# Eight full expert units listed after tile 16 and run right behind the last sums of a graph and expert kernel

## What is computed

```python
edge_index = jnp.stack([src, dst])            # 3125 nodes of 256 numbers; E = 12500 edges are used
x = x + gnn(layernorm(x), edge_index, ...)    # two layers: mean over incoming edges @ W_l + x @ W_r + b
x = x + moe(layernorm(x), ...)                # 8 experts, the best 2 of each row

def moe(tokens, router_w, w1, b1, w2, b2):
    probs = softmax(tokens @ router_w.T)
    rw, re = top_k(probs, 2);  rw = rw / rw.sum(-1)
    out = tokens
    for e in range(8):
        h = gelu(tokens @ w1[e] + b1[e])      # 256 -> 256
        out = out + combine[:, e:e + 1] * (h @ w2[e] + b2[e])
```

## Time and profile before

| | us |
|---|---|
| median of 3 runs (range) | 593.08 (591.64 to 593.94) |
| profiled execution, its own time | 592.88 |
| its span from the first to the last instruction | 591.2 |
| PE busy in the span | 554.3 |
| DVE busy | 364.7 |
| ACT busy | 222.2 |
| POOL busy | 185.5 |

### The profile page before, as it was taken

One profiled execution on the slowest core, in us unless ns is written; L12 is line 12 of the kernel. 1 busy time (PEld: TensorE's weight loads), 2 busy tenths in 40 slices (PEclk: granted clock), 3 DMA queues, 4 the chain that ended last, 5 costly groups with the idle time before them and its releaser, 6 DMA issues.

```text
span 591.2 us, 11509 instructions
## 1 busy us (share of the span) xinstructions
PE 554.3 (94%) x3050; PEld 336.3 (57%) x3051; DVE 364.7 (62%) x1219; ACT 222.2 (38%) x422; POOL 185.5 (31%) x180
## 2 busy tenths in 40 slices
PE   4999999999999999999999999999991499999996
PEld 3555555555555555555445555555551488888885
DVE  5998667667657667663255766767678334444442
ACT  4676845434444434443101100000000155555554
POOL 3751000000000000000040154443356237787887
PEclk9999999999999999999999999999996799999999
DMA  8421211111111111012642146673332757787776
GB/s 259 148 79 60 65 45 54 48 34 54 44 37 55 37 44 54 28 55 53 196 129 80 55 137 200 202 245 126 106 130 97 228 109 118 125 142 129 129 116 92
DMA packets 64343, 61.24 MB, mean 104 GB/s; under 512 B 11281, under 2 KB 62334, under 8 KB 64302
## 3 DMA queue, kind: packets, MB, share of 16 engines
q1 hardware_dynamic: 47422, 44.84, 25.2%
q0 software_dynamic: 11200, 14.40, 13.1%
q10 hardware_dynamic: 5680, 1.49, 1.2%
HBM read 32.34 MB, written 29.30 MB: 104 GB/s over the span
## 4 chain that ended last, share of the span: by engine, by line
PE 69%; DMA 9%; DVE 8%; issue 8%; POOL 4%; SPq 1%; ACT 0%; POOLq 0%; DVEq 0%; ACTq 0%
PE bank L1306 22%; PE counts_ps L1448 8%; PE bank L1459 8%; PE bank L1221 8%; PE bank L1296 7%; PE counts_ps L662 7%; PE counts_ps L1306 4%; POOL xs_dram L593 2%; DMA rows<-in_x 2%; PE counts_ps L1439 2%; DMA xs_dram<-w,onehots 2%; DMA y<-y_dram 2%; PE bank L1211 1%; POOL stat L581 1%; PE bank L1289 1%
## 5 line engine op out<-in xcount | busy, mean ns | idle before, releaser
L1306 PE MATMUL bank<-y,adj 128*128 128x512 f16 x625 | 154.7, 379 | 0.4 <-ACT zt L1519 0.4
L1306 PE MATMUL counts_ps<-y,adj 128*128 128x512 f16 x625 | 144.0, 379 | 2.0 <-DMA y<-y_dram 2.0
L669 ACT ACTIVATE adj<-counts_ps 128x1000 f32 (+1 forms) x80 | 80.2, 1005 | 59.2 <-PE counts_ps L662 59.2
L635 POOL DMA_INDIRECT out<-adj x56 | 88.4, 1578 | 37.9 <-ACT adj L1654 18.5
L1306 PEld LDWEIGHTS counts_ps<-y,adj 128*128 128x128 f16 x625 | 60.7, 101 | 64.7 <-DMA y<-y_dram 4.3
L1306 PEld LDWEIGHTS bank<-y,adj 128*128 128x128 f16 x625 | 57.9, 97 | 59.5 <-issue 13.7
L565 POOL IOTA onehots<- 128x8 int32 x1 | 0.1, 143 | 225.4 <-PE counts_ps L662 225.4
L1448 PE MATMUL counts_ps<-adj 128*128 128x256 f32 x240 | 57.0, 380 | 0.0
L662 PEld LDWEIGHTS counts_ps<-onehots 125*128 125x128 f16 x640 | 42.4, 98 | 23.6 <-ACT adj L669 11.0
L648 DVE TENSOR_TENSOR onehots<-iota,lo_t 125x1024 f16<-125x1024 f16 x80 | 54.7, 684 | 1.8 <-issue 0.9
L1618 ACT ACTIVATE rows<-bank 128x256 f32<-128x256 f32 x25 | 9.6, 384 | 123.0 <-PE bank L1380 123.0
(11 more groups left out here) (237 smaller groups left out, 646.6 us busy)
## 6 DMA issues: line engine op xcount, KB each, us to landing
adj<-xs_dram SPq DMA_DIRECT2D x31, 264.0 KB
rows<-z_dram SPq DMA_DIRECT2D x49, 128.0 KB, 2.1
z_dram<-zt SPq DMA_DIRECT2D x33, 128.0 KB, 1.7
adj<-in_L_ffn_w SPq DMA_DIRECT2D x16, 256.0 KB, 3.2
rows<-in_x SPq DMA_DIRECT2D x24, 128.0 KB
out<-yo SPq DMA_DIRECT2D x24, 128.0 KB
y_dram<-yo SPq DMA_DIRECT2D x23, 128.0 KB, 1.7
y<-y_dram SPq DMA_DIRECT2D x4, 640.0 KB, 6.8
```

The source lines that it names most:

```text
L635: g.indirect_dma_start(out, bass.IndirectOffsetOnAxis(ap=ids[u][:, h:h + 1], axis=0), ye[u][:, h, :], None, bounds_check=N - 1, oob_is_err ...
L669: nc.scalar.activation(adj[:, :, bass.ds(at, GW * WD)].rearrange("p b (h d) -> p b h d", d=WD), counts_ps[:, 2 * (group % 2):2 * (group % ...
L1306: last = te.matmul(to, adj[:, b, t * P:(t + 1) * P], y[:, b, :], start=(b == 0), stop=(b == NT - 1))
```

## The change

A first list of eight units is made from the counts of the first 16 tiles: per expert as many units as are already full, the lowest experts first, until there are eight. DVE counts and lists behind tiles 18 and 19, PE spreads inside tile 21, DVE writes the first entries of the tables. The first two units' rows are loaded, and their weights and shares kept, during tiles 22 and 23. Behind the last matmul of tile 24 PE goes straight on to these eight units, and the routing of the last tiles, the second list (all other units) and the padding stand between their parts on every engine, written out by hand. The loops then run from unit 8 on. The 14 fillers go. The core of the difference follows.

On SP, the loads and paddings (the first two lines stand in tile 22, behind a wait for the scatters of 16 tiles):

```diff
+            load_rows(first_row, 0)
+            load_rows(second_row, 1)
...
+            next_rows(4, row_of(4))
+            row = row_of(5)
+            pad_expert(0)
+            next_rows(5, row)
+            row = row_of(6)
+            pad_expert(1)
+            pad_expert(2)
+            next_rows(6, row)
...
+            sp.wait_ge(S["table"], 2)
+            row = row_of(EARLY)
...
             sp.wait_ge(S["padded"], 16 * NE)
             for q in range(2):
                 sp.wait_ge(scattered[q], 16 * TOPK * len(range(q, NT, 2)))
...
+            next_rows(EARLY, row)
```

On POOL, the last scatters and the early adds:

```diff
+            for t, j in to_scatter[NT - BATCH - 1:FIRST_OF[NB - 1]]:
                 scatter(t, j)
...
             pool.wait_ge(S["table"], 1)
+            pool.wait_ge(S["u_out"], 16 * FIRST_OF[EARLY_BATCH])
+            for q in range(AHEAD):
+                add_half(0, q, True)
+            for t, j in to_scatter[FIRST_OF[NB - 1]:]:
+                scatter(t, j)
+            for q in range(AHEAD, EARLY_ROUNDS * HALVES):
+                add_half(q // HALVES, q % HALVES, True)
```

On DVE, inside the loop over tiles and behind it:

```diff
+                if t == LIST_AT:
+                    dve.wait_ge(S["listed"], 1)
+                    tables(bank[2], EARLY, 0, EARLY, 0)
+                if t == LIST_AT + 2:
...
+                    keep_w1(0, 0)
+                    keep_w1(1, 1)
+                norm_and_sum(t)
+                if t == FIRST_OF[EARLY_BATCH] + 2:
+                    count_first()
+                if t == FIRST_OF[EARLY_BATCH] + 3:
+                    list_first()
...
+                if t == FIRST_OF[NB - 1]:
+                    keep_meta(0, 0, 16)
+                    keep_meta(1, 1, 16)
+                    choose(NB - 2)
+
+            early_unit(2)
+            reached_by_batch()
+            early_unit(3)
+            choose_experts(NB - 1)
+            early_result(0)
+            shares(NB - 1)
+            place(NB - 1)
+            early_unit(4)
+            early_result(1)
+            early_unit(5)
+            early_result(2)
+            list_rest()
+            early_unit(6)
+            early_result(3)
+            dve.wait_ge(S["listed"], 2)
+            tables(bank[0], NTAB, EARLY, NTAB, 2 * EARLY)
+            early_unit(7)
+            early_result(4)
+            dve.wait_ge(S["table"], 2)
+            for i in range(EARLY, EARLY + 3):
+                early_unit(i)
+                early_result(i - 3)
```

On PE and on ACT, behind the last tile:

```diff
+            def early_round(i):
+
+                result(i, i % 2)
+                if i == 0:
+                    score(NT - 1)
+                hidden(i + 2, i % 2)
+                turn_rows((i + 3) % 2, 16 * ((i + 3) // 2 + 1))
+
+            early_round(0)
+            early_round(1)
+            prefix(NB - 1)
+            for i in range(2, 4):
+                early_round(i)
+            list_units(spread, bank[0], 2)
+            early_round(4)
+            pe.wait_ge(S["table"], 2)
+            for i in range(5, EARLY):
+                early_round(i)
...
             turn_rows(2, 0)
...
+            phase3(NT - 1)
+            powers(NB - 1)
+            for i in range(EARLY):
+                if i == 5:
+                    act.wait_ge(S["table"], 2)
+                gelu(i + 2, i % 2)
+                turn_rows(i + 3, (i + 3) % 2)
+                weigh(i, i // UNITS, i % UNITS)
+                if 1 <= i < 5:
+                    pad_experts(act, [NE // 2 + i - 1])
```

More of the change, by code:

```diff
@@ L281, in build @@
         xt_ps = [counts_ps[:, s, :] for s in range(2)]
-        hid_ps = [counts_ps[:, 2 + s, :] for s in range(2)]
+        hid_ps = [counts_ps[:, 3 - s, :] for s in range(2)]
         y_ps = [halves(bank[2 + s][:, :]) for s in range(2)]
@@ L617, in _, with add_half @@
                     scatter(*to_scatter[t - BATCH - 1])
-            for t, j in to_scatter[NT - BATCH - 1:]:
+            def add_half(n, q, full):
+                u, h = q // 2, q % 2
+                before_it = pool.value_load(tab_wi[0:1, bass.ds(n * HALVES + q, 1)], min_val=0, max_val=2 * MAX_PAIRS)
+                pool.wait_ge(landed[q % NLAND], landed_before(n, q))
+                for d in range(1, NLAND):
+                    r = (q - d) % NLAND
+                    pool.wait_ge(landed[r], (before_it + (NLAND - 1 - r)) // NLAND * 16 + 32)
+                pool.wait_ge(S["ye_in"], n * HALVES + (q + 5))
+                pool.sem_inc(S["pool_held"], 1)
+                at = bass.IndirectOffsetOnAxis(ap=ids[u][:, h:h + 1], axis=0)
+                if full:
+                    g.indirect_dma_start(out, at, ye[u][:, h, :], None, compute_op=ALU.add).then_inc(landed[q % NLAND], 16)
+                else:
+                    g.indirect_dma_start(out, at, ye[u][:, h, :], None, bounds_check=N - 1, oob_is_err=False,
+                                         compute_op=ALU.add).then_inc(landed[q % NLAND], 16)
@@ L622, in _ @@
             pool.wait_ge(S["u_out"], 16 * NT)
             rounds = pool.value_load(nround_i[0:1, 0:1], min_val=MIN_ROUNDS, max_val=MAX_ROUNDS)
-            with pool.Fori(0, rounds) as n:
+            with pool.Fori(EARLY_ROUNDS, rounds) as n:
                 for q in range(HALVES):
[L626 to L637, removed]
+                    add_half(n, q, False)
@@ L1095, in place @@
                 v.tensor_copy(slots[:, FIRST_OF[j] * TOPK:(FIRST_OF[j] + BATCH) * TOPK], slot_f).then_inc(S["slots"], 1)
[L1097 to L1101, removed]
-                if t == NT - 1:
-                    place(NB - 2)
-                norm_and_sum(t)
-                if t % BATCH == 0 and 0 < j < NB - 1:
-                    choose(j - 1)
-                if t == FIRST_OF[NB - 1]:
-                    choose(NB - 2)
+            at_p = meta[:, 0:1, NODE_ID - D:NODE_ID - D + 1].rearrange("p t c -> p (t c)")
@@ new lines, in early_result @@
+            def early_result(i):
+                result(i, i // UNITS, i % UNITS)
+            for t in range(NT):
+                x2_and_var(t)
+                j = t // BATCH
+                if t % BATCH == 2 and 0 < j < NB - 1:
+                    place(j - 1)
+                if t == NT - 1:
+                    place(NB - 2)
+                if t == LIST_AT:
+                    dve.wait_ge(S["listed"], 1)
+                    tables(bank[2], EARLY, 0, EARLY, 0)
+                if t == LIST_AT + 2:
+                    dve.wait_ge(S["ew_in"], 16 * 3 * NE)
+                    dve.wait_ge(S["table"], 1)
+                    keep_w1(0, 0)
[5 more added lines that the diff above has]
+                    list_first()
+                if t % BATCH == 0 and 0 < j < NB - 1:
+                    choose(j - 1)
+                if t == FIRST_OF[NB - 1]:
+                    keep_meta(0, 0, 16)
+                    keep_meta(1, 1, 16)
+                    choose(NB - 2)
```

279 lines of the change are left out of this document (183 added, 96 removed).

## The result

| | before | after |
|---|---|---|
| median (range of 4 runs each), us | 593.17 (591.64 to 593.94) | 599.48 (598.02 to 601.55) |
| ratio to before, 95% interval | | 1.0112 (1.0075 to 1.0149) |
| span of the profiled execution, us | 591.2 | 597.2 |
| PE, POOL busy, us | 554.3, 185.5 | 556.3, 184.8 |

The account below looks back on a forecast made before the run. PE (3.92 us a unit) and POOL (3.72) were taken as nearly equal bounds of the tail. Span 591.2 + 0.9 (add 16's lag) + 6.8 (later waits) = 598.9; execution took 1.7 more; forecast 600 us (596 to 605, chance 0.56), whole range 586 to 605.

Parts of the forecast that it names:

- Sums: DVE's added work up to tile 24, less covered waits: last sums end 4.3 us later, at 448.7; bounds 0.9 to 6.
- The chain behind the last sums: DVE's work in order from 454.2 to the end of unit 4's bias at 485.0: 30.8 us.
- load 0.8, copy 0.43, `keep_meta` 0.43: On DVE, weights and row numbers of units 2, 3, 4, 6, 7: 1.66 us each, 8.3 together.
- The gate: ACT's last padding follows `weigh` of unit 4; SP awaits all paddings before loading unit 8, whose rows arrive at 493.0.
- The waits between adds: On POOL, landing waits in the new order: 5.7 us up to add 16, 6.8 behind it.
- the median landing 3.9 + 0.30: On POOL, an add waiting with none in flight starts 4.2 us after the one ahead, 2.3 over 1.86.
- one in flight: On POOL, a wait that allows one earlier add still flying costs 1.1 us, between 0 and 1.6.
- PE sets the end: Rival: adds never have to wait, result 8 comes 6.5 us sooner; 586.4 us (583 to 590), chance 0.22.
- Landings are short: Rival: landing waits on POOL cost less, 3.1 us start to start; no change, 593 us (590 to 596), chance 0.22.
- The other half of that rival: In the no-change case: DVE chain 5 us shorter, waits priced as forecast, 595.6 us; shares that case's chance 0.22.
- The first loads come late: Rival: SP's wait for tile 15's scatters delays units 0 and 1; 601 to 604 us, inside the range, no separate chance.
- The clock: PE pauses over 5 us ahead of unit 8; clock may fall, costing nothing if POOL ends last, otherwise up to 2 us.

Follow-up runs that it names:

- force_before: The kernel before, with the first add of rounds 1 to 6 (adds 8, 16, 24, 32, 40, 48) waiting for all adds ahead: 612.83 us, ratio 1.0318.
- own_before: The kernel before, with adds sent to four destinations in turn and no add waiting for another's landing: 595.0 us, ratio 0.9999.
- own_after: The changed kernel, with adds sent to four destinations in turn and no add waiting for another's landing: 585.3 us, ratio 0.9824.
- gate_after: The changed kernel, with ACT's paddings behind `weigh` of units 1 to 3 and `weigh` of units 6 and 7 ahead of the GELU: ratio 1.0084.

## Why the prediction was right, point by point

**Sums: 2.6 us late, not 4.3.** Mechanism right, term too large. The two `keep_w1` of tile 23 took 1.8 us (440.25 to 442.05 on DVE) where 2.7 were booked, since a register load showed 0.69 and 0.34 of idle instead of 0.96; the two `keep_meta` took 0.7 for 0.9. The other 0.6 were not traced one by one; DVE's waits for POOL's root fell from 5.2 to 3.5 us in all over 395 to 450 us, so that they covered 1.7 where 0.76 was booked.

**The chain behind the last sums: 27.6 us, not 30.8.** From DVE's last work of tile 24 (452.20) to the end of unit 4's bias (479.83). The six copies of weights with row numbers took 6.8 us (booked 9.35), five biases 8.1 (9.5), the last batch 7.0 (5.95; its wait for `prefix` is 1.05 and not 0.2), the rest 6.0 (5.95). The failed step is "load 0.8, copy 0.43, `keep_meta` 0.43" for each copy: ahead of four of the six copies the register load shows as 0.20 to 0.77 us of idle time, and as none ahead of those of units 5 and 7 (468.09 and 477.55), which stand behind a bias and the second tables.

**The gate: unit 8's rows at 487.2, not 493.0.** The gate itself was right: ACT's last padding stands behind `weigh` of unit 4, and SP, DVE and PE wait for it in this order. 5.2 us of the difference is the bias of unit 4. Behind it stands this pair of rows of ACT after:

```profile
481.02 0.38 ACTq L422 DMA_DIRECT2D xs_dram<-biases  x1
481.02 0.91 ACT L1845 ACTIVATE adj<-adj 128x256 f32<-128x256 f32 x2
```

The padding's DMA starts with the `weigh` it stands behind in the program, not 1.6 us later: 1.2 us behind the bias, not 1.9. It landed in 2.2 us, not 3.0; SP's issue and unit 8's rows then took 4.0 us, not 3.1. PE's pause was 3.65 us, where over 5 was named, and result 7 stood at 493.76, not 497.3. Add 10 started at 490.32, below the 493 that the prediction had named as the sign that the chain was priced too high.

**The waits between adds: right places but for two, too cheap.** The table worked out from the counts named adds 14, 16, 26 and 30 with none in flight; all four stand in POOL's timeline above, and 25 and 32 with one. Start to start they are 5.28, 6.12, 4.92 and 5.06 us, where 4.2 was booked. The step that failed is "the median landing 3.9 + 0.30": force_before gives 5.2. The price of one in flight was too low as well: add 25 came 5.51 us after add 23 and 32 came 5.75 after 30, so 1.7 to 2.0 us and not 1.1. One wait was missed: add 12, 4.0 us behind 11, was held by ACT, where `weigh` of unit 6 stands behind the GELU that needs unit 8's rows. It covered the one booked for add 13, which starts 1.85 us behind 12. And of the two waits of the earlier trace rows from which the places were taken as seen, own_before leaves only that of add 15 as a landing wait.

**How the errors met.** Add 10 was 7.0 us early. From there to add 16 it took 20.9 us for the 16.9 booked: 2.1 more at add 12, 1.1 at 14 and 2.0 at 16, 1.1 less at 13. Behind add 16 the waits are 10.0 us for 6.8, of which 1.9 came back because the kernel before had small hiccups in that stretch, the wait of 1.3 ahead of its add 32 among them, which the prediction took to run add on add. -7.0 + 4.0 + 3.2 - 1.9 = -1.7: span 597.2 for 598.9. The mechanism forecast is thus the one that acted, but that 600 us stand beside 599.48 is luck: the front was off by 7.0 us one way and the waits by 7.2 the other. (The prediction's own sum, 598.9 + 1.7, is 600.6.)

**The rivals.** "PE sets the end" did not happen; with the landings out of the way, in own_after, PE sets the pace, and POOL ends some 2.7 us behind it. "Landings are short" is refuted by force_before. There the Trainium skill's rule for a DMA (DMA: Bandwidth & Descriptors, section "Anatomy of one DMA"), about 2.0 us and the bytes, 2.3 us for one add as the prediction estimated from it, is not what the trace shows: 3.9 us to landing in the median, and 5.2 from an add to one that waits for it. The other half of that rival, a chain on DVE 5 us shorter, came true (unit 8's rows were there 5.8 us sooner); its 595.6 us did not follow, because the waits cost more than booked. "The first loads come late" did not happen: `keep_meta` of unit 0 follows at once on DVE at 442.84. The clock was as named: over 483 to 492 us, around the pause, the granted clock is 0.81, and result 6, behind the pause, took 3.41 us where result 8 took 1.89. Result 6 stands on PE ahead of the first weights of unit 8, for whose GELU, and with it ACT, add 12 waited. But in gate_after, where PE's pause is 1.85 us and result 6 takes 1.99, adds 14 and 16 stand at 503.36 and 511.57, no sooner than in the changed kernel (counted from add 0, add 16 is 1.0 us sooner). So the pause and the clock cost little there, about the 0.3% by which that run is faster. ACT's table loads took 1.28 us each again (at 444.95, 453.62 and 457.88).

## What to carry to other kernels

When work is started early because part of it is ready, look at what the rest becomes: here the early units took the long runs, and left remainders that touch the same rows and must wait for each other. The order alone moved this change from 1.1% slower to 0.6% faster. Price a dependent DMA as start to start (landing plus what the issuing queue does behind it), from a place where such a wait is seen or made, and not as the landing alone; and before counting a gain on one engine, force or remove the wait on the next, to see which one sets the end.

## What was not expected of the hardware

- An accumulating indirect DMA that waits for the one ahead starts 5.2 us after it (4.85 to 5.70 in the six of force_before), of which 3.7 to 4.2 are its landing and 1.1 POOL's own queue; without a wait the same queue shows 0.30 between two.
- The four paddings that ACT issues in the changed kernel start before the `weigh` that stands ahead of them has ended, one of them together with it (both at 481.02); their starts are no sign that the work ahead is done.
- A few small loads cost time on an engine's queue: four biases took 3.01 us on ACT's and were hidden, six took 3.92 us and held the next copy for 1.5 us, and with PE's longer wait and lower clock behind it the first store of the next stage came 3.8 us later.
- PE stalls that come back from POOL through the buffers can lower the granted clock: behind one of 2.33 us it is 0.70 over 521 to 525 us and behind one of 2.71 us 0.68 over 555 to 560, while behind one of 2.15 us it stays at 1.00 over 545 to 549.
